# Attention units of a macaron block: the low halves of late weights after the scores' maxima, statistics and ScalarE's normalizations in halves

## The chip, the cores and the metric

The kernel runs on one core of one Trainium2 chip. The metric is the device time of one execution in microseconds. TensorE (PE in the rows) multiplies matrices, ScalarE (ACT) copies and exponentiates, VectorE (DVE) does elementwise work and reductions, GpSimd (POOL) helps, and SyncE (SP) issues the loads. Each engine takes its own instructions in order and waits on semaphores for the others.

## What is computed

A block in three parts on 2048 tokens of width 256 (8 sequences of 256): half a mixture of experts, attention, half a mixture of experts again, each on normalized input. The change lies in the attention:

```python
qi = hadamard((x @ wq_idx).reshape(B, S, Hi, Di))      # 16 index heads
ki = hadamard(x @ wk_idx)
I = einsum('bth,bhts->bts', x @ w_iw, relu(einsum('bthd,bsd->bhts', qi, ki)))
vals, idx = top_k(where(causal, I, NEG), 32)           # which keys each token sees
q, k, v = x @ wq, x @ wk, x @ wv                        # 16 heads, one k and v
p = softmax(scores of q with the 32 chosen k)
out = (p @ v).reshape(B, S, H * hd) @ wo
```

Products of float32 are made from halves: a weight or an activation is split into a high half (rounded for TensorE) and a low half (what is left), and three products of halves stand for one.

## The kernel before

`order()` (line 28) writes out by hand one list of stages. Each engine's block walks the whole list and emits its own part of every stage, so the list is the order of work on every engine at once. `tally` counts the stages, and the waits are made from those counts.

The tokens are worked in 4 groups of 512. In the attention there are 64 units U, 16 to a group (u is the place in the group). A unit takes two heads of one sequence. While unit U runs its attention, units up to 29 also carry one index head of a group two further on. What a unit's stages do, in the order of the list:

- `qi`: TensorE projects the next index head (six matmuls of 512 columns) into bank 0, ScalarE copies it twice (line 1085, `PA<-ps` and `RR<-ps`), VectorE subtracts for the low half (line 1281, `RR<-ps,RR` 128x256) and frees the bank.
- `scores`: TensorE multiplies q with k into banks 1 and 2. VectorE adds the mask and takes the maxima (line 1696, out `SP` and `NB`), which frees banks 1 and 2. ScalarE exponentiates (line 1250), four instructions with their sums.
- `wo` of unit U-3: twelve matmuls of 256 columns into banks 6 and 7.
- `l`: TensorE multiplies the index head with its keys, again into banks 1 and 2 (in the rows the first matmul is line 798, `ps<-PA`), so it waits until VectorE has read the scores. ScalarE takes the positive part into `R` (line 1242), VectorE sums it up (line 1657).
- `q`: the next head of q, in bank 0. `scale`: VectorE's reciprocal (line 1706), GpSimd's multiplications (line 1818). A step of the search for the 32 largest (`drip`, lines 1671 and 1674).
- `pv` of U-2 and `flip_p` of U-1: copies on ScalarE and subtractions of 128x512 and 128x384 on VectorE (line 1281).
- The end of the unit: what the change touches.

What stands at the end of units 0 to 12 before the change:

- `halve(32 + U)`: the dictionary `coming` gives for each late weight (wq 3 to 7, wo 1 to 7) the unit that issues its load and the unit that splits it. A `split` is ScalarE's copy into the high half (`RR<-stage`, line 1085) and at the same place of the list VectorE's subtraction for the low half (`RR<-stage,RR`, line 1281). The loads go through two shelves of the tile `stage`; a load waits until the low half of the weight that had its shelf is done. The splits stand in units 1 to 6 and 7 to 12 (one in each), the loads in units 0 to 11.
- `stats`, `rough` and `moments` of the last group (key "a", columns 12 to 15) at the end of units 1, 3 and 5: VectorE's means and variances (lines 1322, 1325), a first guess of the inverse root, and two steps of Newton.
- `centre` of that group on ScalarE at the end of unit 8, and of the groups with key "q" at the end of units 10 and 26: four instructions in one stage (line 1122). That of key "q" is written into `stage` and waits for all low halves that stand before it in the list.

The last group is transposed (`flip`) in unit 13, those of key "q" in units 14 and 30.

Of the kernel before, what the change touches and what calls it, by code (L numbers as in the profile page):

```python
# [30 lines left out]
def order():  # L31

    def bring(*names):
        return [("bring", q) for q in names]

    def split(eh, el, *names):
        return [("split", q, eh, el) for q in names]

    def high(*names):
        return [("hi", q, "act") for q in names]  # L40

    def low(*names):
        return [("lo", q, "dve") for q in names]
# [5 lines left out]
    def centre(key, g, at, *engines):  # L49
        k = 4 // len(engines)  # L50
        return [("centre", key, g, at, eng, k * i, k) for i, eng in enumerate(engines)]
# [4 lines left out]
    def scatters(n, *groups):  # L56
        return [st for r in range(2) for g in groups for st in
                [("tag", n, g)] * r + [("scatter", n, i, r) for i in range(4 * g, 4 * g + 4)]]

    def marks(n, *groups):  # L60
        return [("mark", n, g, 0) for g in groups]
# [99 lines left out]
    def fill3(s, late):  # L161
# [10 lines left out]
        elif (s, late) == (3, 1):  # L172
# [4 lines left out]
    yield ("attention",)  # L177
    yield from [("project", 0, 0), ("iw", 0), ("qi", 0, 0)]

    coming = {("wq", 0): (1, 3), ("wq", 1): (4, 6), ("wq", 2): (7, 9), ("wq", 3): (32, 33), ("wo", 1): (32, 34),  # L180
              ("wq", 4): (33, 35), ("wo", 2): (34, 36), ("wq", 5): (35, 37), ("wo", 3): (36, 38), ("wq", 6): (37, 39),
              ("wo", 4): (38, 40), ("wq", 7): (39, 41), ("wo", 5): (41, 42), ("wo", 6): (42, 43), ("wo", 7): (43, 44)}

    def halve(k):
        for name, (_, when) in coming.items():
            if k == when:
                yield from split("act", "dve", name)
        for name, (when, _) in coming.items():
            if k == when:
                yield from bring(name)  # L190

    def early(h):
        if h in (5, 9):
            yield ("stats", "a", h - 1, 4, h - 1)
        if h == 10:
            yield ("rough", "a", 4, 8, 4)
        if h == 11:
            yield ("moments", "a", 4, 8, 4)
        if h == 12:
            yield from centre("a", 1, 4, "act")  # L200
        if h == 13:
            yield ("flip", "a", 1, 3, 4)
        if h == 14:
            yield from centre("a", 2, 8, "act")
        yield from halve(h)
# [9 lines left out]
    def begin_topk(g):  # L215
        left.extend((what, g, b, r) for b in range(2) for what, r in [("best", r) for r in range(4)] + [("mask", 0)])
        return [("causal", g, 0), ("causal", g, 1)]

    def drip(k):
        out = left[:k]  # L220
        del left[:k]
        return out
# [3 lines left out]
    def ahead_to(U):  # L226
        while nextq[0] <= min(U, 63):
            yield ("q", nextq[0])
            nextq[0] += 1
# [13 lines left out]
    yield from drip(1) + [("project", 0, 2), ("iw", 2), ("qi", 2, 0)] + drip(1)  # L243
    yield from ahead_to(1)
    yield from begin_topk(1)
    yield from [("values", 0), ("l", 2, 0), ("qi", 2, 1)]

    later = scatters(1, 0, 1)[:8] + [None, None] + scatters(1, 0, 1)[8:]

    def prepare(U):  # L250

        stats = lambda g, i: [("stats", "m1", 4 * g + 2 * i, 2, 4 * g + 2 * i)]
        rest = lambda g, p: [(p, "m1", 4 * g, 4, 4 * g)]
        half = lambda g, i: [("half", "m1", g, i, 1 + i)]
        first, second, third = [], [], []
        for i, U0 in enumerate((20, 21, 35, 37, 51, 52)):
            if U == U0:
                first += stats(i // 2, i % 2)
        for i, U0 in enumerate((22, 39, 52)):
            if U == U0:  # L260
                first += rest(i, "rough")
        for i, U0 in enumerate((23, 41, 53)):
            if U == U0:
                first += rest(i, "moments")
        for g, begin in ((0, 24), (1, 42), (2, 53)):
            if U in (begin, begin + 1):
                third += centre("m1", g, 4 * g, "act", "act")[U - begin:U - begin + 1]
        for i, U0 in enumerate((34, 36, 44, 45, 55, 55)):
            if U == U0:
                second += half(i // 2, i % 2)  # L270
        for g, U0 in enumerate((46, 46, 56)):
            if U == U0:
                first.append(("logits", 1, g, 0 if g == 1 else 5))
        for q, begin in ((0, 47), (1, 57)):
            if U == begin:
                first.append(("pick", 1, q))
            elif U == begin + 1:
                first.append(("sel", 1, q))
            elif U == begin + 2:
                first += [("shift", 1, q), ("count", 1, q, 5), ("place", 1, q, 5)]  # L280
            elif U == begin + 3:
                first += [("choose", 1, q)] + (marks(1, 2) if q else marks(1, 0, 1))
                if q:
                    later.extend(scatters(1, 2)[:4] + [None, None] + scatters(1, 2)[4:])
        if U == 31:
            third.append(("blank", 1))
        elif 32 <= U < 40:
            third += [("clear", k) for k in (2 * U - 64, 2 * U - 63) if k < CLEARS]
        elif U == 62:
            third += [("refill", x) for x in range(3)]  # L290
        if U >= 50:
            third += [st for st in later[:2] if st]
            del later[:2]
        for i in range(3):
            if U == 32 + i:
                third += bring(("sh", 1, i))
            elif U == (50, 52, 58)[i]:
                third.append(("hi", ("sh", 1, i), "act"))
            elif U == (54, 56, 61)[i]:
                first.append(("lo", ("sh", 1, i), "dve"))  # L300
        return first, second, third

    for U in range(64):
        g, u = divmod(U, 16)
        gi, hi = divmod(U + 34, 16)
        idx = gi < NG
        first, second, third = prepare(U)
        if 0 < u < 14 and idx:
            yield ("qi", gi, hi)
        elif idx and (u == 15 or U == 16):  # L310
            yield ("qi", gi, hi - 1)
        yield ("scores", U)
        if U >= 32 and not first:
            yield from drip(1)
        yield from first
        if u == 15 and g + 1 < NG:
            yield ("project", 1, g + 1)
        if u == 14 and g < 2:
            yield ("flip", "q", g + 1, 3, 4)
        if U == 13:  # L320
            yield ("flip", "a", 3, 3, 4)
        if U >= 3:
            yield ("wo", U - 3)
        if u == 1 and U > 1:
            yield from [("pv", U - 2), ("values", g)]
        if U == 0:
            yield from ahead_to(2)
        if idx:
            if u == 14:
                yield from [("project", 0, gi), ("iw", gi)]  # L330
            elif u == 15:
                yield ("l", gi, 0)
            elif u == 0:
                yield from [("l", gi, 1), ("qi", gi, 2)]
            else:
                yield ("l", gi, hi)
        if 0 < u < 14 and U < 32 or u == 15 or U in (32, 33, 49):
            yield from ahead_to(U + 2 if U < 33 else U + 3)
        yield ("scale", U)
        if U < 32 and u < 13 and u != 1 and (u == 3 or u % 4 != 3):  # L340
            yield from drip(1)
        if U >= 2 and u != 1:
            yield ("pv", U - 2)
        yield from second
        if U:
            yield ("flip_p", U - 1)
        yield from ahead_to(U + 2 if U < 32 else U + 3)
        if idx and u == 0:
            yield ("l", gi, 2)
        yield from halve(32 + U)  # L350
        if U in (1, 3, 5):
            yield (("stats", "rough", "moments")[U // 2], "a", 12, 4, 12)
        if U == 8:
            yield from centre("a", 3, 12, "act")
        if u == 10 and g < 2:
            yield from centre("q", g + 1, 4 * g + 4, "act")
        if u == 13 and g < 2:
            yield from begin_topk(g + 2)
        yield from third
# [148 lines left out]
def macaron_kernel(nc, x, cst_in, row_in, gw_in, wsh_in, wex_in, wqi_in, ws_in, wiw_in, wq_in, wo_in, out):  # L508
# [7 lines left out]
    AX = mybir.AxisListType  # L516

    stages = list(order())
    at, whole = tally(stages)
    ctx = ExitStack()  # L520
# [1451 lines left out]
```

How the kernel before makes its waits and increments, by code:

```python
    def wait_ge(self, sem, value):  # L502
        if value > self.had.get(sem.name, 0):
            self.e.wait_ge(sem, value)
            self.had[sem.name] = value
# [206 lines left out]
        def settled(lane, m, g):  # L712
            num = min(8 * BATCHES[m][[g in q for q in BATCHES[m]].index(True)][-1] + 8 + NE - 1, NT)
            for k in range(4):
                lane.wait_ge(S[f"yst{k}"], 16 * (m * len(range(k, NT, 4)) + len(range(k, num, 4))))
# [68 lines left out]
        @block.tensor  # L785
# [34 lines left out]
            for st in stages:  # L820
                kind, a, n = st[0], st[1:], at[st]
                def free(bank):
                    t.wait_ge(S[f"bank{bank}"], n.get(("bank", bank), 0))
                    t.wait_ge(S["xres"], n.get(("emptied", bank), 0))
                if kind in ("flip", "half"):
                    key, g = a[0:2]
                    for done in CENTRED[key, g]:
                        t.wait_ge(*done)
                    t.wait_ge(S["ident"], 16)
                    src = NORMED[buffer(key, g)]
                    for dc, bank in enumerate(a[2:4]) if kind == "flip" else [a[2:4]]:
# [4 lines left out]
                        ins.then_inc(S["xt"], 1)  # L838
                elif kind == "warm":
                    t.wait_ge(S["warm"], 1)
                    for i in range(a[0]):
# [1 line left out]
                elif kind == "logits" and a[0] == 0:  # L843
                    m, g, bank = a
                    t.wait_ge(S["gates"], 2)
                    free(bank)
# [430 lines left out]
            def after(value):  # L1277
                t.wait_ge(S["dve"], value)
```

## Time and profile before

| | |
|---|---|
| median of 3 timed runs | 929.7 us (929.33 to 930.57) |
| profiled execution | 927.29 us, its span 925.5 us |
| TensorE's matmuls busy | 881.0 us, 95% of the span |
| VectorE, ScalarE, GpSimd busy | 685.4, 547.3, 394.6 us |
| mean granted TensorE clock | 0.992 of full speed |
| attention units 0 to 63 | from about 294 to 780 us of the span |

In rows of the timeline the first number is the start, the second the length, both in us; in brackets stands how long the engine was idle before it and which instruction ended the wait. A number after x counts merged instructions. Lines 1085 and 1281 are helpers, so the tiles tell which stage an instruction belongs to.

### The profile page before, as it was taken

Reading aid. Unit: us, or ns where it says so; the run is one execution under the profiler, and the core shown is the slowest. Engines: PE = TensorE matmul, PEld = TensorE weight load, DVE = VectorE, ACT = ScalarE, POOL = GpSimd, SP = SyncE. Lnnn points to the kernel's source line nnn. Section 1 sums busy time; section 2 is a strip of 40 time slices with the busy share of each in tenths; the row PEclk is TensorE's granted clock in tenths of the full one; section 3 lists DMA queues with packets and bytes.
Section 4 is the critical chain, followed back from the end, with each engine's and each line's share of the span. In section 5 each row is a group of like instructions: output and inputs, shape, how many; then the busy total and the mean of one; then the engine's idle time right before and its main releaser. Section 6 shows DMA issues by size and latency. Waiting matters only on the chain.

```text
span 925.5 us, 19094 instructions
## 1 busy us (share of the span) xinstructions
PE 881.0 (95%) x5846; PEld 787.8 (85%) x5847; DVE 685.4 (74%) x2388; ACT 547.3 (59%) x1586; POOL 394.6 (43%) x525
## 2 busy tenths in 40 slices
PE   8799999899999899989999999999999998999997
PEld 3478999788887788888899988999989997789996
DVE  7886667768797777766788676878678675847786
ACT  4454555457665566676666766667567774425562
POOL 0683687410000333323243344455428686126672
PEclk9999999999999999999999999999999999999999
DMA  9243896550000011000000000998000024624475
GB/s 348 94 138 126 311 352 218 120 115 23 1 1 1 15 33 35 13 23 2 1 2 1 1 1 1 307 308 223 1 1 35 30 89 171 270 70 127 133 243 173
DMA packets 52451, 96.26 MB, mean 104 GB/s; under 512 B 5824, under 2 KB 37184, under 8 KB 50304
## 3 DMA queue, kind: packets, MB, share of 16 engines
q1 hardware_dynamic: 44672, 73.20, 24.8%
q0 software_dynamic: 7680, 21.83, 7.5%
q8 instruction: 50, 0.82, 0.4%
q14 instruction: 49, 0.40, 0.2%
HBM read 44.99 MB, written 50.02 MB: 103 GB/s over the span
## 4 chain that ended last, share of the span: by engine, by line
PE 75%; DVE 15%; ACT 6%; issue 3%; DMA 0%; POOL 0%; DVEq 0%; ACTq 0%
PE ps L793 35%; PE ps L798 32%; DVE RR L1281 4%; PE ps L1042 3%; PE ps L951 2%; PE ps L921 2%; ACT SP L1250 2%; DVE PA L1657 1%; ACT RR L1085 1%; DVE st L1322 1%; DVE SP L1696 1%; PE ps L836 1%; DVE xl L1281 1%; DVE PA L1281 1%; DVE X L1281 1%
## 5 line engine op out<-in xcount | busy, mean ns | idle before, releaser
L1818 POOL TENSOR_SCALAR SP<-SP,RC 128x128 f32<-128x128 f32 (+1 forms) x256 | 193.6, 775 | 261.3 <-DVE RC L1706 261.1
L1281 DVE TENSOR_TENSOR RR<-ps,RR 128x256 fp32r<-128x256 f32 (+2 forms) x322 | 158.3, 525 | 74.3 <-ACT RR L1085 73.7
L798 PE MATMUL ps<-RR,RA 128*128 (+1 forms) x1002 | 176.6, 315 | 5.4 <-DVE RA L1281 4.2
L1250 ACT ACTIVATE SP<-SP,NB 128x128 f32<-128x128 f32 (+1 forms) x256 | 113.5, 444 | 76.0 <-DVE NB L1696 75.8
L1085 ACT ACTIVATE RR<-ps 128x256 fp32r<-128x256 f32 (+2 forms) x322 | 137.0, 469 | 28.3 <-PE ps L793 26.4
L798 PEld LDWEIGHTS ps<-RR,RA 128*128 128x128 f32 x1002 | 143.3, 189 | 11.8 <-issue 9.1
L793 PE MATMUL ps<-xh,RR 128*128 128x512 f32 x368 | 135.3, 412 | 0.0
L1657 DVE SCALAR_TENSOR_TENSOR PA<-R,IW,PA 128x128 f32<-128x128 f32 x240 | 84.8, 415 | 41.0 <-ACT R L1242 40.9
L1786 POOL DMA_INDIRECT yr<-FA,IDX x78 | 84.4, 1082 | 53.4 <-ACT FA L1085 16.7
L798 PE MATMUL ps<-RR 128*128 128x256 f32 x768 | 103.7, 285 | 3.0 <-DVE RR L1281 3.0
L798 PEld LDWEIGHTS ps<-RR 128*128 128x128 f32 x768 | 96.9, 191 | 4.0 <-DVE RR L1281 3.6
L793 PE MATMUL ps<-xh,RT 128*128 128x512 f32 x272 | 96.6, 401 | 0.2 <-DVE RR L1281 0.2
L793 PEld LDWEIGHTS ps<-xh,RR 128*128 128x128 f32 x368 | 71.3, 194 | 13.9 <-DVE RR L1281 0.2
L1085 ACT ACTIVATE QF<-ps 128x256 f32<-128x256 f32 x96 | 36.9, 384 | 66.4 <-PE ps L793 66.4
L793 PE MATMUL ps<-KIH,RR 128*128 128x256 f32 x256 | 76.2, 325 | 0.0
L793 PE MATMUL ps<-KH,RR 128*128 128x256 f32 x256 | 75.5, 323 | 0.0
L793 PE MATMUL ps<-xl,RR 128*128 128x512 f32 x184 | 74.2, 403 | 0.0
L1281 DVE TENSOR_TENSOR RA<-ps,RA 128x256 fp32r<-128x256 f32 x156 | 64.8, 417 | 8.8 <-ACT RA L1085 8.8
L1085 ACT ACTIVATE RA<-ps 128x256 fp32r<-128x256 f32 x156 | 59.4, 384 | 19.9 <-PE ps L921 19.6
L793 PE MATMUL ps<-RR,VH 128*128 128x512 f32 (+1 forms) x256 | 66.2, 340 | 0.1
L1242 ACT ACTIVATE R<-ps 128x384 f32<-128x384 f32 x128 | 58.8, 483 | 8.2 <-DVE VL L1281 2.7
L793 PEld LDWEIGHTS ps<-xh,RT 128*128 128x128 f32 x272 | 51.1, 188 | 10.2 <-DVE RR L1281 0.4
(238 smaller groups left out, 1867.2 us busy)
## 6 DMA issues: line engine op xcount, KB each, us to landing
xg<-stage SPq DMA_DIRECT2D x15, 1161.0 KB, 15.3
FA<-xg SPq DMA_DIRECT2D x78, 129.0 KB, 2.7
kept<-RR SPq DMA_DIRECT2D x8, 1216.0 KB
RR<-kept SPq DMA_DIRECT2D x8, 1216.0 KB, 10.8
X<-yr POOLq DMA_DIRECT2D x6, 512.0 KB, 5.6
RAW<-yr SPq DMA_DIRECT2D x6, 512.0 KB, 5.3
RAW<-wex_in SPq DMA_DIRECT2D x8, 352.0 KB, 9.7
RAW<-wsh_in SPq DMA_DIRECT2D x6, 384.0 KB, 9.1
```

The lines of the kernel that those rows point to most:

```text
L793: ins = e.matmul(o, a, c, start=first and i == 0, stop=last and i == len(seq) - 1, skip_group_check=True)
L798: return e.matmul(o, a, c, start=start, stop=stop, skip_group_check=True)
L921: ins = e.transpose(PS[bank][:, 128 * dc:128 * dc + 128], MOE[m].XS[j % NX][:, 128 * dc:128 * dc + 128], ident[:])
L951: ins = e.transpose(PS[bank][:, 128 * z:128 * z + 128], MOE[m].G[:, j % 2, 128 * z:128 * z + 128], ident[:])
L1042: ins = e.transpose(PS[3 + i][:, 128 * z:128 * z + 128], SP[:, k, i, 128 * z:128 * z + 128], ident[:])
L1085: return e.activation(o, i, ACT.Copy)
L1242: e.activation(R[:, b, :], PS[1 + b][:, 0:384], ACT.Relu).then_inc(S[f"bank{1 + b}"], 1)
L1250: ins = e.activation(SP[:, k, i, o:o + w], SP[:, k, i, o:o + w], ACT.Exp, scale=-1.0, bias=NB[:, k, 2 * i + z:2 * i + z + 1], accum_out=SM ...
L1281: return e.tensor_tensor(o, p, q, alu)
L1657: ins = e.scalar_tensor_tensor(Is, r, iw, Is, ALU.mult, ALU.add)
L1786: e.indirect_dma_start(out=YR[m], out_offset=bass.IndirectOffsetOnAxis(ap=IDX[:, j % 8:j % 8 + 1], axis=0), in_=MOE[m].YS[:, j % 4, :], in ...
L1818: ins = e.tensor_scalar(SP[:, k, i, o:o + w], SP[:, k, i, o:o + w], RC[:, k, 2 * i + z:2 * i + z + 1], None, ALU.mult)
```

## The change

The late weights leave `coming` for a list `pieces` in order of use. The load of the first stands before the units. At the end of unit U (0 to 11) ScalarE makes the high half of piece U; VectorE makes its low half in unit U+1 directly behind the scores' maxima. The load of piece U+2 is issued at the end of unit U (pieces 1 and 2 in unit 0). The last group's `stats` become two stages of two columns, in units 1 and 2, `rough` goes to unit 4 and `moments` to unit 6, all behind the maxima. ScalarE's `centre` of the last group is made in two halves at the end of units 8 and 9, those of key "q" in two halves at the end of units 11 and 12, and 27 and 28. No instruction is added or removed.

```diff
-    coming = {("wq", 0): (1, 3), ("wq", 1): (4, 6), ("wq", 2): (7, 9), ("wq", 3): (32, 33), ("wo", 1): (32, 34),
-              ("wq", 4): (33, 35), ("wo", 2): (34, 36), ("wq", 5): (35, 37), ("wo", 3): (36, 38), ("wq", 6): (37, 39),
-              ("wo", 4): (38, 40), ("wq", 7): (39, 41), ("wo", 5): (41, 42), ("wo", 6): (42, 43), ("wo", 7): (43, 44)}
+    coming = {("wq", 0): (1, 3), ("wq", 1): (4, 6), ("wq", 2): (7, 9)}
+    pieces = [("wq", 3), ("wo", 1), ("wq", 4), ("wo", 2), ("wq", 5), ("wo", 3), ("wq", 6), ("wo", 4), ("wq", 7), ("wo", 5),
+              ("wo", 6), ("wo", 7)]
...
-    yield from [("values", 0), ("l", 2, 0), ("qi", 2, 1)]
+    yield from [("values", 0), ("l", 2, 0), ("qi", 2, 1)] + bring(pieces[0])
...
         first, second, third = prepare(U)
+        if 1 <= U <= len(pieces):
+            first = low(pieces[U - 1]) + first
+        if U in (1, 2):
+            first.append(("stats", "a", 10 + 2 * U, 2, 10 + 2 * U))
+        elif U in (4, 6):
+            first.append((("rough", "moments")[U // 5], "a", 12, 4, 12))
...
-        yield from halve(32 + U)
-        if U in (1, 3, 5):
-            yield (("stats", "rough", "moments")[U // 2], "a", 12, 4, 12)
-        if U == 8:
-            yield from centre("a", 3, 12, "act")
-        if u == 10 and g < 2:
-            yield from centre("q", g + 1, 4 * g + 4, "act")
+        if U < len(pieces):
+            yield from high(pieces[U])
+        for k in {0: (1, 2), 11: ()}.get(U, (U + 2,)):
+            if k < len(pieces):
+                yield from bring(pieces[k])
+        if U in (8, 9):
+            yield from centre("a", 3, 12, "act", "act")[U - 8:U - 7]
+        if u in (11, 12) and g < 2:
+            yield from centre("q", g + 1, 4 * g + 4, "act", "act")[u - 11:u - 10]
```

## Rows read from the trace of the kernel before

**Rows 1.** The page, its first part: busy us, share of the span, instructions.
```profile
PE 881.0 (95%) x5846; PEld 787.8 (85%) x5847; DVE 685.4 (74%) x2388; ACT 547.3 (59%) x1586; POOL 394.6 (43%) x525
```

**Rows 2.** Waits of TensorE, 286 to 775 us: total us, times, longest us.
```profile
PE ps L798 <- DVE NB L1696: 10.1, 7, 2.8
```

**Rows 3.** Timeline of TensorE: the first matmuls of `l` in eleven units.
```profile
304.97 0.46 PE L798 MATMUL ps<-PA 128*128 128x128 f32 x2 [0.69 <-DVE NB L1696]
313.43 0.53 PE L798 MATMUL ps<-PA 128*128 128x128 f32 x2 [2.46 <-DVE NB L1696]
323.46 0.46 PE L798 MATMUL ps<-PA 128*128 128x128 f32 x2
333.04 0.46 PE L798 MATMUL ps<-PA 128*128 128x128 f32 x2 [1.11 <-DVE NB L1696]
351.62 0.46 PE L798 MATMUL ps<-PA 128*128 128x128 f32 x2 [1.65 <-DVE NB L1696]
377.73 0.46 PE L798 MATMUL ps<-PA 128*128 128x128 f32 x2 [0.95 <-DVE NB L1696]
397.50 0.46 PE L798 MATMUL ps<-PA 128*128 128x128 f32 x2 [2.84 <-DVE NB L1696]
405.80 0.39 PE L798 MATMUL ps<-PA 128*128 128x128 f32 x2
...
497.81 0.39 PE L798 MATMUL ps<-PA 128*128 128x128 f32 x2
506.04 0.39 PE L798 MATMUL ps<-PA 128*128 128x128 f32 x2
539.53 0.46 PE L798 MATMUL ps<-PA 128*128 128x128 f32 x2 [0.43 <-DVE NB L1696]
```

**Rows 4.** Windows around the lowered clock: us, busy by engine, PEclk, DMA share, GB/s.
```profile
310.30:313.70 3.40, 0.94 (x9) 0.77 (x8) 3.37 (x17) 0.59 (x3) 1.79 (x3) 1.00 0.33 80
313.70:317.10 3.40, 3.40 (x14) 3.09 (x13) 1.54 (x6) 2.35 (x10) 0.00 (x0) 0.50 0.01 2
665.30:668.70 3.40, 3.40 (x15) 3.21 (x15) 0.41 (x3) 0.00 (x0) 2.86 (x4) 0.50 0.00 0
```

**Rows 5.** Timeline of VectorE: the last group's statistics, `rough` and `moments`, ends of units 1, 3, 5.
```profile
310.62 1.39 DVE L1322 BATCH_NORM_STATS2 st<-X 128x6 f32<-128x256 f32 x4
312.05 0.38 DVE L1325 BATCH_NORM_AGGREGATE mv<-st 128x2 f32<-128x6 f32 x4
330.83 0.16 DVE L1284 TENSOR_SCALAR nt<-mv 128x4 f32<-128x4 f32 x1
331.84 0.17 DVE L1344 SCALAR_TENSOR_TENSOR nt<-nt 128x4 f32<-128x4 f32 x1
349.24 0.15 DVE L1281 TENSOR_TENSOR nt<-nt 128x4 f32<-128x4 f32 x1
350.43 0.17 DVE L1347 SCALAR_TENSOR_TENSOR nt<-mv,nt 128x4 f32<-128x4 f32 x1
```

**Rows 6.** Timeline of ScalarE: end of units 10 and 11, and the copy after it.
```profile
393.74 2.08 ACT L1122 ACTIVATE stage<-X,nt 128x256 f32<-128x256 f32 x4 [1.78 <-DVE RR L1281]
402.61 0.65 ACT L1085 ACTIVATE RR<-stage 128x512 fp32r<-128x512 f32 x1
403.42 0.38 ACT L1085 ACTIVATE PA<-ps 128x256 f32<-128x256 f32 x1 [0.16 <-PE ps L793]
```

**Rows 7.** Timeline of VectorE: low half of a weight (unit 11), maxima, next sums (unit 12).
```profile
403.54 0.68 DVE L1281 TENSOR_TENSOR RR<-stage,RR 128x512 fp32r<-128x512 f32 x1
404.68 0.42 DVE L1696 CUSTOM_DVE_ANT_0 SP<-ps,PA 128x256 f32<-128x256 f32 x1
407.42 1.41 DVE L1657 SCALAR_TENSOR_TENSOR PA<-R,IW,PA 128x128 f32<-128x128 f32 x4 [1.76 <-ACT R L1242]
```

**Rows 8.** DMA issues, KB, us to landing: quiet (280 to 410 us), then busy (90 to 170 us).
```profile
stage<-wo_in SPq DMA_DIRECT2D x6, 256.0 KB, 2.6
...
stage<-wqi_in SPq DMA_DIRECT2D x8, 256.0 KB, 4.2
```

More of the change, by code:

```diff
@@ L178, in order, with halve @@
     yield from [("project", 0, 0), ("iw", 0), ("qi", 0, 0)]
-    coming = {("wq", 0): (1, 3), ("wq", 1): (4, 6), ("wq", 2): (7, 9), ("wq", 3): (32, 33), ("wo", 1): (32, 34),
-              ("wq", 4): (33, 35), ("wo", 2): (34, 36), ("wq", 5): (35, 37), ("wo", 3): (36, 38), ("wq", 6): (37, 39),
-              ("wo", 4): (38, 40), ("wq", 7): (39, 41), ("wo", 5): (41, 42), ("wo", 6): (42, 43), ("wo", 7): (43, 44)}
-    def halve(k):
+    coming = {("wq", 0): (1, 3), ("wq", 1): (4, 6), ("wq", 2): (7, 9)}
+    def halve(h):
         for name, (_, when) in coming.items():
-            if k == when:
+            if h == when:
                 yield from split("act", "dve", name)
         for name, (when, _) in coming.items():
-            if k == when:
+            if h == when:
                 yield from bring(name)
+    pieces = [("wq", 3), ("wo", 1), ("wq", 4), ("wo", 2), ("wq", 5), ("wo", 3), ("wq", 6), ("wo", 4), ("wq", 7), ("wo", 5),
+              ("wo", 6), ("wo", 7)]
     def early(h):
```

## The prediction, made before the changed kernel was built or run

> **What bounds the kernel now.** I read the page's busy times first. TensorE's matmuls fill 881.0 us, 95% of the span [rows 1]. The change adds and removes no matmul, so all it can win is TensorE's idle time and time at a lowered clock. The second view is the list of TensorE's waits over the attention units. One line carries nearly everything: 7 waits, 10.1 us, for VectorE's maxima, which free banks 1 and 2 for the index product `l` [rows 2]. The third view is TensorE's timeline, which says in which units those waits lie. The reader is to see that they stand at the start of `l` in units 1, 2, 4, 6, 9, 11 and 27 (0.69, 2.46, 1.11, 1.65, 0.95, 2.84 and 0.43 us) [rows 3]. All but the first follow a unit whose end holds one of the pieces the change moves: statistics (end of unit 1), `rough` (3), `moments` (5), `centre` (8, 10 and 26). The fourth view, the windows, shows that after the 2.46 us wait the clock was granted at 0.50 for 3.4 us [rows 4], which is 1.2 instead of 2.4 GHz.
>
> The mechanism can be read from rows 5 to 7. At the end of a unit the order on VectorE is subtractions, a weight's low half, the extra piece, then the next unit's low half of `qi`, then the maxima. Whatever stands there pushes the maxima back one for one, and TensorE, after the twelve matmuls of `wo`, has nothing else to do. On the other side of the maxima VectorE waits anyway: 1.76 us for ScalarE, which first exponentiates and then makes `R` [rows 7]. The same wait stands in nearly all of units 1 to 12; one row stands for them.
>
> **What a unit costs when nothing waits.** From `l` to `l` an undisturbed unit takes 506.04 - 497.81 = 8.23 us, and it holds the same matmuls as units 3 to 11 [rows 3].
>
> **The change part by part.**
>
> *Units 3 to 12.* From 323.46 to 405.80 lie nine units in 82.34 us [rows 3]. Nine undisturbed ones would take 9 x 8.23 = 74.07 us. The difference, 8.27 us, is what VectorE's and ScalarE's extras cost there. The gaps of the four rows add to 6.55 us. The rest, 1.72 us, are shortfalls without a gap in brackets: a matmul that waited has lost its overlap with the one before it, and units with only a low half at their end are late by some tenths too. Moving the low halves removes those as well.
>
> *Unit 2.* Unit 2, like unit 1, has no `wo` ahead of `l`, so a wait is left even without extras: I take that of unit 1, 0.69 us. Gain 2.46 - 0.69 = 1.77 us [rows 3].
>
> *The clock.* From 313.43 to 323.46 a unit took 10.03 us [rows 3] with no gap in it: 1.80 us over 8.23. That is the stretch at 0.50 behind the gap [rows 4]. With 0.69 us instead of 2.46 us of idle time I take it to go away, since the gap of 0.69 us in unit 1 has no such stretch behind it. Bounds: 0 to 1.8 us of gain.
>
> The Trainium skill, page "TensorE: Matmul & The Clock Gate", section "Part 1: The HAM clock gate", has a monitor set the clock by how busy TensorE was lately. The stretch after the gap agrees [rows 4]. The other one does not so plainly: at 665.3 us the clock is at 0.50 too, and no wait of TensorE lies before it [rows 4]. By the page alone the first would go with the gap, as in my sum.
>
> *Unit 27.* 0.43 us of gap, and about 0.2 us of lost overlap as in the row of unit 9. Gain 0.6 us; ScalarE's half (below) finds idle time there.
>
> *What goes into the 1.76 us behind the maxima.* A low half is 0.68 us [rows 7]. With half of the statistics, (1.39 + 0.38) / 2 = 0.89 us [rows 5], units 1 and 2 take 1.57 us: covered. `rough` runs from 330.83 to 332.01, 1.18 us; with a low half 1.86 us, 0.10 over. `moments` runs from 349.24 to 350.60, 1.36 us; with a low half 2.04 us, 0.28 over [rows 5]. Queued behind are VectorE's sums and the low half of `q`, which frees bank 0 for the next `qi`. What is over has a unit's rest to be made good, because the low half of 0.68 us is gone from the end. I take 0; if it is not made good it is 0.4 us in all. Were there no cover at all, twelve low halves and the extras would be 12 x 0.68 + 1.77 + 1.18 + 1.36 = 12.5 us.
>
> *ScalarE's halves.* Four normalizations took 2.08 us, so a half is 1.04 us. At the end of units 8, 9 and 11 it follows a weight's high half. ScalarE had only 0.16 us of idle time between that high half (402.61) and the next copy (403.42) [rows 6]. So the copy of `qi` comes some 0.7 to 0.9 us later, and with it the maxima. In unit 12 the first pair's maxima ended at 405.10 and `l` began at 405.80, 0.70 us later, part of which TensorE needs to wake up [rows 3, 7]. What is left over is an estimated 0.15 to 0.35 us in each of three places: I take 0.5 us in all. At the end of units 12, 27 and 28 no high half stands before it. In unit 10 ScalarE also waited 1.78 us for VectorE's low half of a weight before it could overwrite `stage` [rows 6]. After the change the low halves waited for stand half a unit earlier, so that wait goes; it is part of the 2.84 us.
>
> *High halves a unit earlier.* In unit 0 a new one, 0.65 us, falls into the time before the next `qi` copy. In unit 12 one goes. Nothing in the sum.
>
> *The loads.* On SyncE only loads stand in this part of the list, so nothing is held up behind a waiting one. Each of the last three (wo 5, 6, 7) uses the shelf of its forerunner, and can start only behind that one's low half: just after the maxima. Its high half stands at the end of the same unit. In unit 12 the maxima ended at 407.42 - 1.76 = 405.66, so a low half would end at 406.34 [rows 7]; the high half of unit 11 began at 402.61 [rows 6], so one a unit later begins near 410.8: some 4.5 us for the load. A load took 2.6 us here, and 4.2 us where the queues were full [rows 8]. I take 2.6, as this stretch is quiet; both are covered.
>
> *Sum.* 8.27 + 1.77 + 1.80 + 0.6 - 0.5 = 11.9 us. Everything after these units waits on what they produce and on no fixed time, so the gain should reach the end. The sum is made against the profiled execution: 927.29 - 11.9 = 915.4 us. The timed runs' median lies 2.4 us above it, so from that: 929.7 - 11.9 = 917.8 us.
>
> **Rivals.**
>
> *The slow stretch stays or moves.* The waits go, but a stretch at 0.50 appears somewhere else, since units 0 to 2 keep gaps and since the one at 665.3 us follows no wait. Then the gain is 10.1 us and the time 919.6 us. On the other side the stretch at 665.3 may go too with the shifted start, for another 1.7 us: 916.1 us.
>
> *The work behind the maxima is not covered.* If ScalarE's `R` comes much earlier once the maxima are early, VectorE's idle time shrinks and the moved work pushes the sums, the low half of `q` and the next `qi`. If half of the moved 12.5 us lands on the path, the gain is about 5.7 us: 924.0 us. If all of it, nothing is won: 929.7 us, within 0.2%. Against it: ScalarE exponentiates for most of the 1.76 us whenever it starts, so the time moves along with the maxima.
>
> *The last three loads come late (slower).* If wo 5, 6 and 7 don't land by the end of their unit, ScalarE stands still with the copy of `qi` behind it, and so do the maxima and `l`. The cover is 4.5 us. To cancel 11.9 us a load would need 4.5 + 11.9 / 3 = 8.5 us. At 10 us each it would cost 3 x 5.5 = 16.5 us, so 934.3 us. Rows 8 show 2.6 and 4.2 us, half of that at most, so it is unlikely.
>
> **How the numbers follow.** Forecast 917.8 us, chance 0.60. Slow stretch stays, 919.6 us: 0.14. One more goes, 916.1 us: 0.12. Half covered, 924.0 us: 0.06. No cover, 929.7 us: 0.04. Late loads, 934.3 us: 0.04. The range goes from 914.3 (both stretches gone and no cost of ScalarE's halves, with a little room) to 921.3 us (slow stretch stays and the small costs are doubled or the unit's shortfalls remain). It leaves out 0.14. About 0.2%, 1.9 us, is what a measurement of this kernel can tell from no change. Faster by over that: 0.92; within: 0.04; slower: 0.04.
>
> **What would show each step.** In the profile after, TensorE's waits for VectorE's maxima should fall from 10.1 us to about 2, with 0.7 us in units 1 and 2 and none above 0.4 us elsewhere. From `l` to `l` units 3 to 12 should take 8.2 to 8.5 us. VectorE's low halves from `stage` should stand directly behind line 1696, and the idle time before line 1657 should fall from 1.76 us to about 1 in plain units and to nothing in units 4 and 6. The clock should stay at 1.00 around 314 us. No wait of ScalarE for a load of wo should appear. The prediction is wrong if TensorE's waits come back for bank 0 (low half of `q` late) or if units 8 to 12 stay above 9 us.

## The result, and the profile after

The changed kernel takes 917.3 us (median of 4 runs, 914.7 to 918.9) against 929.5 us before (928.7 to 930.6). The ratio is 0.9865, with a 95% interval of 0.9837 to 0.9894. The forecast was 917.8 us, in a range of 914.3 to 921.3. Run again on the chip of the last experiments it took 916.6 us (4 runs) against 928.4, ratio 0.9874 (0.9855 to 0.9892).

The profiled execution of the changed kernel took 914.69 us with a span of 912.9 us. It is the fastest of its four, as the profiled one of the kernel before (927.29 us) was faster than its timed ones.

The page's first part, and TensorE's waits over the attention units (286 to 775 us: total us, times, longest). These answer to [rows 1, 2]. The line numbers are 9 higher than before (807 for 798, 1290 for 1281, 1705 for 1696).

```profile
PE 878.3 (96%) x5846; PEld 785.2 (86%) x5847; DVE 685.6 (75%) x2388; ACT 547.0 (60%) x1586; POOL 393.8 (43%) x525
```

```profile
PE ps L807 <- ACT PA L1094: 1.4, 1, 1.4
PE ps L807 <- DVE NB L1705: 1.4, 2, 0.7
```

TensorE's waits for the maxima fell from 10.1 to 1.4 us. The two left are those of units 1 and 2, which have no `wo` ahead of the index product. The wait of 1.4 us for ScalarE (`PA`) lies in unit 0 and was there before too. TensorE's timeline shows them, and the same instruction in units 3, 4 and 12 with no wait. They answer to [rows 3].

```profile
305.80 0.46 PE L807 MATMUL ps<-PA 128*128 128x128 f32 x2 [0.70 <-DVE NB L1705]
312.50 0.46 PE L807 MATMUL ps<-PA 128*128 128x128 f32 x2 [0.69 <-DVE NB L1705]
320.81 0.39 PE L807 MATMUL ps<-PA 128*128 128x128 f32 x2
329.03 0.39 PE L807 MATMUL ps<-PA 128*128 128x128 f32 x2
...
395.39 0.46 PE L807 MATMUL ps<-PA 128*128 128x128 f32 x2
```

From unit 1 to unit 12 it is 395.39 - 305.80 = 89.59 us, where it was 405.80 - 304.97 = 100.83 us [rows 3]. That is 11.24 us of the 12.6 us by which the spans differ.

VectorE in unit 4 shows what now stands behind the maxima: the low half (line 1290, `RR<-stage,RR`), then `rough`, then the sums (line 1666). The rows answer to [rows 5, 7].

```profile
328.58 0.42 DVE L1705 CUSTOM_DVE_ANT_0 SP<-ps,PA 128x256 f32<-128x256 f32 x1
328.93 0.69 DVE L1290 TENSOR_TENSOR RR<-stage,RR 128x512 fp32r<-128x512 f32 x1
329.53 0.16 DVE L1293 TENSOR_SCALAR nt<-mv 128x4 f32<-128x4 f32 x1
...
330.55 0.17 DVE L1353 SCALAR_TENSOR_TENSOR nt<-nt 128x4 f32<-128x4 f32 x1
330.76 1.40 DVE L1666 SCALAR_TENSOR_TENSOR PA<-R,IW,PA 128x128 f32<-128x128 f32 x4
332.47 0.43 DVE L1290 TENSOR_TENSOR RR<-ps,RR 128x256 fp32r<-128x256 f32 x1 [0.31 <-ACT RR L1094]
```

The 1.76 us of idle time [rows 7] are filled to the last tenth, and the low half of `q` still waits 0.31 us for ScalarE afterwards: nothing was pushed. In a plain unit (10) the idle time has shrunk to 1.15 us:

```profile
379.06 0.69 DVE L1290 TENSOR_TENSOR RR<-stage,RR 128x512 fp32r<-128x512 f32 x1
380.89 1.41 DVE L1666 SCALAR_TENSOR_TENSOR PA<-R,IW,PA 128x128 f32<-128x128 f32 x4 [1.15 <-ACT R L1251]
```

ScalarE at the end of unit 11: high half, half of the normalization, and the `qi` copy straight behind it, without idle time. The rows answer to [rows 6].

```profile
392.07 0.65 ACT L1094 ACTIVATE RR<-stage 128x512 fp32r<-128x512 f32 x1
392.59 1.09 ACT L1131 ACTIVATE stage<-X,nt 128x256 f32<-128x256 f32 x2
393.58 0.39 ACT L1094 ACTIVATE PA<-ps 128x256 f32<-128x256 f32 x1
```

The loads land as quickly as before (2.6 us in [rows 8]), and ScalarE waits for none of them:

```profile
stage<-wo_in SPq DMA_DIRECT2D x6, 256.0 KB, 2.6
stage<-wq_in SPq DMA_DIRECT2D x4, 256.0 KB, 2.7
```

The windows of TensorE's clock (the third number from the end) show 1.00 where [rows 4] have 0.50: around unit 2, and also in and behind the router's narrow products. These run from 650.2 to 653.8 us now. Before, they ran from 661.6 to 665.2 us, and the stretch at 0.50 lay right behind them.

```profile
312.40:315.80 3.40, 3.30 (x19) 2.95 (x20) 3.16 (x13) 3.08 (x12) 0.53 (x1) 1.00 0.27 80
315.80:319.20 3.40, 3.40 (x25) 3.12 (x24) 3.37 (x12) 2.72 (x7) 2.58 (x4) 1.00 0.00 0
650.00:655.00 5.00, 5.00 (x47) 5.00 (x46) 2.32 (x14) 1.86 (x8) 0.53 (x1) 1.00 0.02 5
655.00:660.00 5.00, 5.00 (x35) 4.51 (x34) 2.42 (x7) 2.02 (x5) 2.46 (x4) 1.00 0.00 0
```

### The profile page after: what moved, and what is told of

It reads as the page before. It is cut to its first block, busy times and chain, and to the rows that moved or that the text cites. A ratio compares the mean times of both kernels' runs of the same rounds, so it can differ in the third digit from the quotient of the medians.

```text
span 912.9 us, 19095 instructions
## 1 busy us (share of the span) xinstructions
PE 878.3 (96%) x5846; PEld 785.2 (86%) x5847; DVE 685.6 (75%) x2388; ACT 547.0 (60%) x1586; POOL 393.8 (43%) x525
## 4 chain that ended last, share of the span: by engine, by line
PE 83%; DVE 10%; ACT 3%; issue 2%; DMA 0%; POOL 0%; DVEq 0%; ACTq 0%
PE ps L802 41%; PE ps L807 34%; PE ps L1051 4%; PE ps L960 2%; DVE RR L1290 2%; PE ps L930 2%; DVE st L1331 1%; PE ps L845 1%; ACT RR L1094 1%; DVE PA L1290 1%; DVE xl L1290 1%; ACT SP L1259 1%; DVE PA L1666 1%; DVE X L1290 1%; DVE FA L1290 1%
## 5 line engine op out<-in xcount | busy, mean ns | idle before, releaser
L807 PEld LDWEIGHTS ps<-RR,RA 128*128 128x128 f32 x1002 | 143.4, 189 | 12.6 <-issue 10.0
L802 PEld LDWEIGHTS ps<-xh,RT 128*128 128x128 f32 x272 | 51.1, 188 | 10.1 <-DVE RR L1290 0.4
```

Source lines behind the costliest of these rows:

```text
L802: ins = e.matmul(o, a, c, start=first and i == 0, stop=last and i == len(seq) - 1, skip_group_check=True)
L807: return e.matmul(o, a, c, start=start, stop=stop, skip_group_check=True)
```

## The experiments

Each is read by one measure, the time from the index product of one unit to that of the next. It is worked out from the starts of the same matmul in each kernel's timeline, as from [rows 3]. This is needed because differences of a few us can't be read from the timed medians. Those of e5, e6, e9, e7, e10 and e12 are of one run each: 918.3, 924.9, 923.2, 921.5, 919.0 and 920.0 us. The first four ran on another chip, on which the kernel before took 942.3 us (31 runs, 935.4 to 949.3) and TensorE's clock was lowered more often in the first 80 us. On every chip, units in which nothing waits take 8.22 to 8.24 us.

Time in us from the index product of the unit named to the next, and in all from unit 1 to unit 12:

| unit | before | changed | e1 | e2 | e3 | e4 | e5 | e6 | e9 | e7 | e8 |
|---|---|---|---|---|---|---|---|---|---|---|---|
| 1 | 8.46 | 6.70 | 7.66 | 6.76 | 8.47 | 6.75 | 6.69 | 6.72 | 6.72 | 6.70 | 6.64 |
| 2 | 10.03 | 8.31 | 8.30 | 8.47 | 9.85 | 8.48 | 8.32 | 8.30 | 8.32 | 8.31 | 8.15 |
| 3 | 9.58 | 8.22 | 9.10 | 8.48 | 9.50 | 8.47 | 8.24 | 8.79 | 8.31 | 8.23 | 8.23 |
| 4 | 8.47 | 8.23 | 8.30 | 8.47 | 8.47 | 8.47 | 8.44 | 8.85 | 9.66 | 8.22 | 8.23 |
| 5 | 10.11 | 8.23 | 9.43 | 8.82 | 10.11 | 8.83 | 8.24 | 9.21 | 8.71 | 8.23 | 8.22 |
| 6 | 8.47 | 8.22 | 8.31 | 8.48 | 8.48 | 8.48 | 9.02 | 8.86 | 10.05 | 8.23 | 8.23 |
| 7 | 8.30 | 8.23 | 8.22 | 8.30 | 8.30 | 8.30 | 8.24 | 8.32 | 8.56 | 8.22 | 8.23 |
| 8 | 9.34 | 8.36 | 9.33 | 9.33 | 8.39 | 8.39 | 8.36 | 8.78 | 8.37 | 8.36 | 8.23 |
| 9 | 8.47 | 8.43 | 8.31 | 8.48 | 8.47 | 8.47 | 8.44 | 8.86 | 8.93 | 10.08 | 8.22 |
| 10 | 11.30 | 8.30 | 9.33 | 11.30 | 8.47 | 8.47 | 8.32 | 8.84 | 8.75 | 9.06 | 8.23 |
| 11 | 8.30 | 8.36 | 8.30 | 8.30 | 9.61 | 9.60 | 8.36 | 8.44 | 8.64 | 9.98 | 8.23 |
| 1 to 12 | 100.83 | 89.59 | 94.59 | 95.19 | 98.12 | 92.71 | 90.67 | 93.97 | 95.02 | 93.62 | 88.84 |

### One part alone

**e1, the weights alone.** The changed kernel without the moves of the statistics and the normalizations.

```diff
-        if U in (1, 2):
-            first.append(("stats", "a", 10 + 2 * U, 2, 10 + 2 * U))
-        elif U in (4, 6):
-            first.append((("rough", "moments")[U // 5], "a", 12, 4, 12))
...
+        if U in (1, 3, 5):
+            yield (("stats", "rough", "moments")[U // 2], "a", 12, 4, 12)
+        if U == 8:
+            yield from centre("a", 3, 12, "act")
+        if u == 10 and g < 2:
+            yield from centre("q", g + 1, 4 * g + 4, "act")
```

> Of the change only the late weights are moved (loads, high halves, low halves behind the maxima); statistics, rough, moments and the normalizations stand as before. My theory (each extra costs what it pushes the next unit's maxima beyond about 0.55 us of slack that the moved low half leaves): over the changed kernel about 1.0 us in unit 2, 0.7 after rough, 0.9 after moments, 0.8 and 0.9 after the two normalizations (the 1.8 us wait of ScalarE for a low half is gone already) and 0.65 in unit 27, in all 5 us: 922 us, or 924 with a stretch at half clock in unit 2. Rival (only the extras were late, the low halves cost nothing where they stood): no gain over the kernel before but the wait of 1.8 us, 927.5 us.

Measured: 94.59 us, 5.00 over the changed kernel. The steps are 0.96 us (unit 1), 0.88 (3), 1.20 (5), 0.97 (8) and 1.03 (10), and 0.66 in units 26 and 27. From unit 1 to unit 28 that makes 5.58 us, where 5 were expected: `rough` and `moments` cost 0.2 and 0.3 us more than I had put them at. So the weights' move alone brings 100.83 - 94.59 = 6.24 us of the 11.24. Only 0.57 of it lies in plain units (4, 6, 7 and 9). Units 1, 3 and 5 give 1.96, since their extras no longer queue behind a low half, unit 10 gives 1.97, since its normalization no longer waits for one, and unit 2 gives 1.73, its time at half clock, which a gap of that length doesn't bring in every execution (see e12). The rival falls. The median was 939.5 against 942.3 us, ratio 0.9958 (0.9913 to 1.0003).

**e2, the statistics alone.** The kernel before with `stats`, `rough` and `moments` where the change has them.

```diff
         first, second, third = prepare(U)
+        if U in (1, 2):
+            first.append(("stats", "a", 10 + 2 * U, 2, 10 + 2 * U))
+        elif U in (4, 6):
+            first.append((("rough", "moments")[U // 5], "a", 12, 4, 12))
...
-        if U in (1, 3, 5):
-            yield (("stats", "rough", "moments")[U // 2], "a", 12, 4, 12)
```

> Of the change only statistics, rough and moments are moved behind the maxima; weights and normalizations stand as before. Theory: the gaps ahead of the index product in units 2, 4 and 6 go (1.77, 1.1 and 1.64 us), with them the stretch at half clock in unit 2 (1.8 us), the rest stays: 6.3 us gained, 923.2 us. Rival (the stretch at half clock has nothing to do with the 2.46 us gap): 4.5 us gained, 925.0 us, and the clock at 0.50 near 314 us of the profile.

Measured: 95.19 us, 5.64 less than before (expected 6.3). Unit 1 gives 1.70, unit 2 with its clock 1.56, unit 3 1.10 and unit 5 1.29. Unit 5 stays at 8.82 us, not 8.47, because the step of the search in that unit is the longer one, and the low half at the end meets it. No stretch at half clock lies behind unit 2. The median was 938.8 us, ratio 0.998 (0.9928 to 1.0031).

**e3, the halves alone.** The kernel before with the change's two `centre` places.

```diff
-        if U == 8:
-            yield from centre("a", 3, 12, "act")
-        if u == 10 and g < 2:
-            yield from centre("q", g + 1, 4 * g + 4, "act")
+        if U in (8, 9):
+            yield from centre("a", 3, 12, "act", "act")[U - 8:U - 7]
+        if u in (11, 12) and g < 2:
+            yield from centre("q", g + 1, 4 * g + 4, "act", "act")[u - 11:u - 10]
```

> Of the change only ScalarE's normalizations are halved and set one unit later; all else as before. Theory: the first pair gains 0.7 us and unit 27 0.65 us, but the pair of units 11 and 12 now waits twice for a low half at the end of its own unit (1.8 us each), so its 3.07 us become about 3.4: in all 1 us gained, 928.6 us, no difference that can be measured. Rival (halving alone removes the normalizations' price of 4.9 us): 925 us.

Measured: 2.7 us less from unit 1 to 12, of which the next interval gives back 1.5: it takes 10.62 us, and 9.13 before. From unit 10 to unit 13 it is 28.70 us, and 28.73 before, and the interval that starts at unit 13 is longer by 0.39 us. Halving the normalization of key "q" brings nothing as long as each half waits for a low half at its unit's end. In units 26 and 27, where no low half stands, it brings 0.65 us. From unit 1 to unit 28 the gain is 1.5 us, where 1 was expected. ScalarE's waits, 395 to 430 us of this kernel:

```profile
ACT SP L1250 <- DVE NB L1696: 3.9, 3, 1.8
ACT stage L1122 <- DVE RR L1281: 3.1, 2, 2.1
```

The second row is that wait: once 1.78 us before [rows 6], now twice, 3.1 us together. The pair of units 8 and 9, which waits for no low half, gained 0.95 us. The median was 941.5 us, ratio 0.9995 (0.9948 to 1.0043).

**e4, only the place of the low halves undone.**

```diff
-        if 1 <= U <= len(pieces):
-            first = low(pieces[U - 1]) + first
...
             yield from high(pieces[U])
+            yield from low(pieces[U])
```

> The changed kernel with each low half put back to the end of a unit, directly behind its own high half; all else as changed. Theory: some 0.2 us in each of the plain units 3 to 8 and 10, 0.4 in unit 2, and ScalarE's first half of the normalization in unit 11 waits 1.8 us for that unit's low half again: 3.3 us over the changed kernel, 920.6 us. Rival (the place of the low halves does not matter once the extras are gone): 917.3 us within half a microsecond.

Measured: 92.71 us, 3.12 over the changed kernel (expected 3.3). Plain units take 8.47 instead of 8.23 us, unit 5 takes 8.83, and unit 11 takes 9.60 because the normalization waits again. Place alone is worth 3.1 us here. The median was 934.0 us, 0.9917 (0.9869 to 0.9966) of the kernel before on that chip. The changed kernel itself has no run there.

The parts have to be added up to the first index product behind unit 13, where e3 has paid back what it gained in unit 10. Up to there (130.06 us before) they give 6.59, 5.65 and 0.84 us, 13.1 in all, and the change gives 11.53. e1 and e2 both remove the stretch at half clock of unit 2, 1.6 to 1.7 us, which counts twice in the 13.1. Beside that there is overlap both ways: without the low half at the end the extras cost less, and ScalarE's halves of key "q" bring nothing in unit 11 until it is gone.

### How much the place behind the maxima covers

**e5, three more instructions there.** In units 3 to 12 three statistics instructions, result unused, ahead of the low half.

```diff
+        if 3 <= U <= 12:
+            first = [("pad", U, 3)] + first
...
+                if kind == "pad":
+                    after(own[0])
+                    for i in range(a[1]):
+                        then(e.bn_stats(PAD[:, i, :], X[:, 12, :]))
```

> The changed kernel with three more statistics instructions on VectorE (1.08 us, their result unused) in each of units 3 to 12, directly behind the maxima and ahead of the low half. Theory (what stands behind the maxima is covered up to about 2.4 us): plain units hold 1.7 us there and stay at 8.2 to 8.4 us from one index product to the next; units 4 and 6, with rough and moments too, hold 2.9 to 3.1 us and grow by about 0.5 us each: 1 us over the changed kernel's profile in all. Rival (VectorE's total work is the bound now): 10 x 1.08 = 10.8 us over it.

Measured: 1.08 us over the changed kernel, though VectorE is busy 9.4 us longer (695.0 and 685.6 us on the pages). Plain units stay at 8.24 us. Unit 4 grew by 0.21 and unit 6 by 0.80.

**e6, the same instructions at the unit's end.**

```diff
+        if 3 <= U <= 12:
+            yield ("pad", U, 3)
```

> The same three instructions in the same units, but at the unit's end, where statistics, rough and moments stood before. Theory: each plain unit grows by 1.08 less 0.55 us of slack, about 0.6 us, those that end with half a normalization by about 0.3: 5 us over the changed kernel's profile, shown as TensorE waiting for the maxima at the start of the index product. Rival (place does not matter): the same as with the instructions behind the maxima.

Measured: 4.38 us over up to unit 12. The table holds nine of the ten ends; what stands at the end of unit 12 costs another 0.75 us in the interval that starts at unit 13. Up to the first index product behind it, ten times the same work costs 1.1 us in the one place and 5.2 us in the other (5 expected). A plain unit grows by 0.57 us (unit 3), not by the whole 1.08: about 0.5 us at the unit's end is slack. Unit 5, with the longer step of the search, grows by 0.98. TensorE's waits, 318 to 400 us, for e6 and then for e5:

```profile
PE ps L810 <- DVE NB L1712: 3.0, 7, 0.7
```

```profile
PE ps L805 <- DVE RR L1293: 0.5, 1, 0.5
```

**e9, six instructions behind the maxima.** The same edit as e5 with 6 for 3.

> Six more statistics instructions (2.16 us) behind the maxima in units 3 to 12, with the low half 2.8 us. Theory: the cover of about 2.4 us is passed; what gets late is the low half of q, so TensorE waits for bank 0 at the next index projection (line 802, ps<-xh), 0.3 to 0.4 us in plain units and about 1.5 us in units 4 and 6: 5.5 us over the changed kernel's profile. Rival (the cover ends at the 1.76 us of idle time): 10 x 1.0 plus the extras, 12 us.

Measured: 5.43 us over up to unit 12, and 0.69 in the next interval, together 6.1 where 5.5 were expected. Here the cover is passed, and the waits have another address (318 to 425 us):

```profile
PE ps L805 <- DVE RR L1293: 3.2, 5, 1.5
```

It is the projection (line 805, `ps<-xh`), which waits for bank 0. In unit 4 VectorE's queue shows why: with pads, low half and `rough` the sums begin 331.94 - 328.36 = 3.6 us after the last maxima, and the low half of `q` behind them.

```profile
327.94 0.42 DVE L1712 CUSTOM_DVE_ANT_0 SP<-ps,PA 128x256 f32<-128x256 f32 x1
328.28 2.05 DVE L1312 BATCH_NORM_STATS2 PAD<-X 128x6 f32<-128x256 f32 x6
330.25 0.67 DVE L1293 TENSOR_TENSOR RR<-stage,RR 128x512 fp32r<-128x512 f32 x1
...
331.94 1.40 DVE L1673 SCALAR_TENSOR_TENSOR PA<-R,IW,PA 128x128 f32<-128x128 f32 x4
333.27 0.41 DVE L1293 TENSOR_TENSOR RR<-ps,RR 128x256 fp32r<-128x256 f32 x1
```

```profile
333.74 0.50 PE L805 MATMUL ps<-xh,RT 128*128 128x512 f32 x1 [1.16 <-DVE RR L1293]
```

So the cover is more than the idle time of 1.76 us: 1.8 us of work is free (plain units of e5), 2.7 to 2.9 us cost 0 to 0.5 us (plain units of e9, unit 4 of e5), and 3.1 us (unit 6 of e5) cost 0.8.

### The late loads

**e7.** The loads of wo 5, 6 and 7 also wait for the reciprocal of the unit in which their high half stands.

```diff
+                        if name in (("wo", 5), ("wo", 6), ("wo", 7)):
+                            t.wait_ge(S["rc"], name[1] + 5)
```

> The changed kernel, but the loads of wo 5, 6 and 7 wait in addition for the reciprocal of the unit in which their high half stands, which comes 2.8 us after the low half they waited for. Theory (the late loads had over 1 us to spare): the load lands about 1.6 us after ScalarE gets to the high half; units 9 and 11, whose slack half a normalization uses already, grow by 1.6 us each and unit 10 by 0.8: 4 us over the changed kernel's profile. Rival (the loads were just in time in the changed kernel): 3 x 2.8 = 8.4 us over it.

Measured: 4.03 us over the changed kernel; units 9, 10 and 11 grew by 1.65, 0.76 and 1.62 us. ScalarE's waits, 360 to 400 us, show the mechanism of the slower rival:

```profile
ACT RR L1094 <- DMA stage<-wo_in: 4.5, 3, 1.5
```

Counted from the index product of their unit the three loads start 3.1, 3.1 and 3.5 us later than in the changed kernel (that of wo 5 at 4.1 instead of 1.0 us). ScalarE waits 1.5, 1.5 and 1.4 us, so they had 1.5 to 2.1 us to spare. Each microsecond beyond costs about a microsecond where half a normalization has used up the slack. The changed kernel's own trace has somewhat less, because one load took longer to land. From issue to high half it has 4.1, 4.1 and 4.4 us, and the loads land after 2.6, 3.1 and 2.5 us: 1.5, 0.9 and 1.9 us are to spare. The slowest of them, 378 to 382 us:

```profile
stage<-wo_in SPq DMA_DIRECT2D x1, 256.0 KB, 3.1
```

The rival's mechanism is real; its condition isn't met.

### The clock

**e10 and e12, the gap of unit 2 brought back.** The same kernel twice: seven statistics instructions at the end of unit 1.

```diff
+        if U == 1:
+            yield from [("pad", U, 4), ("pad", U, 3)]
```

> The changed kernel with seven statistics instructions (result unused) at the end of unit 1, which bring back a gap of about 2.5 us ahead of the index product of unit 2, and nothing else. Theory (the gap caused the stretch at half clock): a stretch at 0.50 of 3.4 us follows and unit 2 takes 10 us instead of 8.3, 3.5 us in all. Rival (the stretch had another cause or depends on where the gap falls in time): no stretch, unit 2 at 8.3 us, 1.8 us in all.

> The same kernel as e10 again, a second execution under the profiler. Theory: as in e10, a stretch at half clock behind the gap in both. Rival (it depends on where the gap falls in time): one of the two profiles, or neither, shows it.

Measured: in both the gap ahead of unit 2 is 2.4 us and unit 1 takes 8.39 us, 1.69 more. In e10 a stretch at half clock follows: the matmuls of 256 columns take 0.41 us in place of 0.28, and unit 2 takes 9.90 us.

```profile
312.41 0.28 PE L805 MATMUL ps<-KH,RR 128*128 128x256 f32 x1
315.08 0.68 PE L810 MATMUL ps<-PA 128*128 128x128 f32 x2 [2.39 <-DVE NB L1712]
...
315.77 0.41 PE L805 MATMUL ps<-KIL,RR 128*128 128x256 f32 x1
...
317.69 0.63 PE L805 MATMUL ps<-xl,RR 128*128 128x512 f32 x1
318.12 0.85 PE L805 MATMUL ps<-xh,RR 128*128 128x512 f32 x2
318.81 0.40 PE L805 MATMUL ps<-xl,RR 128*128 128x512 f32 x1
```

In e12 there is none, and unit 2 takes 8.31 us. With the kernel before and e3, three of the four profiles with this gap have the stretch. The longest gap of all, 2.84 us in unit 11, has none behind it in either of the two profiles that hold it (before and e2). In the profiles without these gaps the clock stays at 1.00 in these units. So the gap is what brings the stretch, but not in each execution, and what decides it isn't shown. The theory of e12 (a stretch in both) failed and its rival held.

### A version meant to be better

**e8.** Normalizations in quarters, and the two gaps of units 1 and 2 filled with work that stood behind the index product.

```diff
-        if U in (8, 9):
-            yield from centre("a", 3, 12, "act", "act")[U - 8:U - 7]
-        if u in (11, 12) and g < 2:
-            yield from centre("q", g + 1, 4 * g + 4, "act", "act")[u - 11:u - 10]
+        if 6 <= U <= 9:
+            yield from centre("a", 3, 12, "act", "act", "act", "act")[U - 6:U - 5]
+        if u in (10, 11, 12) and g < 2:
+            yield from centre("q", g + 1, 4 * g + 4, "act", "act", "act", "act")[u - 10:(u - 9 if u < 12 else 4)]
...
+        if U == 1:
+            yield ("flip_p", 0)
+        if U == 2:
+            yield ("pv", 0)
```

> A version meant to beat the changed kernel: ScalarE's normalizations of the last group in quarters at the ends of units 6 to 9, those of key q as one, one and two at the ends of units 10 to 12 and 26 to 28; the transposes of unit 1 and the p times v product of unit 2 stand ahead of the index product. Theory: a quarter (0.5 us) fits the slack, so units 8 to 11 fall from 8.30-8.43 to 8.23 us (0.5 us), and the two gaps of 0.7 us in units 1 and 2 are filled but for 0.1 (1.25 us): from the index product of unit 1 to that of unit 12 about 88.4 instead of 89.6 us, and 0.6 us before or in it: 1.7 us below the changed kernel. Rival (the copies that move ahead of R on ScalarE and VectorE push the sums): no difference.

> The changed kernel once more, on the same chip as the others of this call, as the base for them and a second profile. Theory: from the index product of unit 1 to that of unit 12 again 89.6 us; what differs from one execution to the next lies in the stretches at half clock outside these units. 12 us below the kernel before.

Measured: 88.84 us from unit 1 to 12, 0.75 less than the changed kernel's 89.59, which e11 repeated (89.58). The quarters bring their 0.53 us in full, as every unit from 8 to 11 takes 8.22 or 8.23. Filling the gaps brings 0.2 us of the 1.25 expected. The wait only moved, to the next projection:

```profile
317.41 0.50 PE L806 MATMUL ps<-xh,RT 128*128 128x512 f32 x1 [0.69 <-DVE RR L1294]
```

In time the two can't be told apart: 917.7 us (916.1 to 918.5) for e8 and 916.6 us (915.4 to 917.6) for the changed kernel, 4 runs each. e8's profile has one stretch at half clock more than e11's outside the units. That such stretches are what hides 0.75 us in the timed runs isn't shown.

## Why the prediction was right, point by point

**The mechanism** was as told. Work at the unit's end pushes the maxima and TensorE with them; behind the maxima it costs nothing up to 1.8 us. e5 and e6 show it with the same instructions in both places, e4 by undoing the place alone. One sentence of it was wrong: work at the end does not push "one for one". A low half of 0.68 us there costs 0.24 us in a plain unit (e4, unit 3), three statistics of 1.08 us cost 0.57 (e6). The sum didn't suffer, since it was made from measured intervals and not from lengths of instructions.

**The sum of the units.** For units 1 to 11 I had 1.77 + 1.80 + 8.27 - 0.5 = 11.34 us. Measured: 11.24.

- Unit 2's wait: 1.77 expected, 8.46 - 6.70 = 1.76 measured.
- The undisturbed unit of 8.23 us held in units 3 to 7.
- ScalarE's halves: 0.5 us expected. Units 8, 9, 10 and 11 stand 0.13, 0.20, 0.07 and 0.13 us over 8.23, together 0.53, and e8 brings all four to 8.23.
- `rough` and `moments` over the idle time by 0.1 and 0.3 us: taken at nothing, and nothing it was.
- Unit 27: 0.6 expected, 0.66 measured (units 26 and 27).

**The clock** is the step that was less sure than its place in the sum said. I took 1.8 us to go away, and in the profile 1.72 did (unit 2, 10.03 and 8.31 us). But e12 shows that the gap has no such stretch in some executions, so the kernel before need not pay it each time. The 1.8 us is a price paid in three of four profiles. The error is hidden by what the prediction didn't have.

**What it didn't have.** The interval that starts at unit 13 is 0.37 us shorter. I had noted that a high half leaves unit 12 ("In unit 12 one goes"), and put it at nothing; the low half leaves the end of that unit too. That end stands ahead of the transposes of key "q", and TensorE's wait for VectorE there shrinks (before, then after):

```profile
421.03 1.06 PE L836 MATMUL ps<-ident,stage 128*128 128x128 f32 x8 [0.36 <-DVE RR L1281]
```

```profile
410.33 1.06 PE L845 MATMUL ps<-ident,stage 128*128 128x128 f32 x8 [0.16 <-DVE RR L1290]
```

e1 and e4, whose unit 12 ends without these halves too, take 19.75 and 19.73 us in this interval like the changed kernel (19.73); e2, where they stand, takes 20.09 like the kernel before. The interval of unit 12 is 0.08 longer.

Outside these units the two profiles differ in what comes and goes by execution. Behind unit 28 the changed kernel is 1.23 us shorter, as the stretch at 665 us [rows 4] is missing. Up to unit 1 it is 0.83 us later. Its additional stretch at half clock at 24 us is not the reason: behind it, at 31.70 and 31.68 us, the same matmul starts in both. The lag builds up between 93 and 140 us, in the first part's experts, at a granted clock of 1.00 in both profiles. In the ten profiles outside e1 to e4 the index product of unit 1 starts anywhere from 304.8 to 309.8 us; why isn't shown. The sum closes: 11.24 - 0.08 + 1.04 + 1.23 - 0.83 = 12.60 us, where 1.04 is units 13 to 27. So the terms of the units were right (11.9 told, 11.24 + 0.66 = 11.90 measured). That the median came within half a microsecond of the forecast is partly luck: the four runs spread over 4.2 us, and the terms not told add up to 0.70 us in the profile.

**The rivals.** "The slow stretch stays or moves" came true in part: one at 24 us is new, the one at 665 us is gone. The latter is missing in three profiles (the changed kernel, e11 and e10) and there in the other eleven. e10 and e12 are the same kernel and differ in it, so it comes and goes by execution. That the change has no part in it isn't shown: both profiles of the changed kernel lack it, and the one profile of the kernel before has it. The lack of cover didn't occur; e9 shows that it sets in about 1 us later than the idle time suggests. Late loads didn't occur. I had put the cover of a load at 4.5 us against 2.6 of landing, 1.9 to spare; it was 0.9 to 1.9, so the loads were up to 1 us nearer to being late than I thought.

**In the expectations of the experiments** the theory of e12 was wrong (a stretch in both executions). The other misses were smaller: e1 (5.58 for 5), e2 (5.64 for 6.3), where I had not seen that unit 5 has the longer step of the search, e3 (1.5 for 1), e9 (6.1 for 5.5), and e8, where I reckoned with one wait of TensorE and not with the one behind it.

## What to carry to other kernels

In a list order shared by all engines, look for the place where an engine waits anyway for a neighbour that is still at work on what it just got, and put loose work there. Work at the end of a round stands ahead of what the busiest engine needs first. Cost each piece by what it pushes, not by its length: the same 1.08 us of VectorE's work cost 0.1 us a unit behind the maxima and 0.5 us at the end. A normalization split in pieces only helps if no piece waits for something that is made at the same late place.

## What the runs showed of the hardware that was not expected

- A matmul that had to wait costs more than its gap: the unit behind it is 0.07 us longer (8.30 and not 8.23), and about 0.16 us of overlap with the matmul before is lost (e1, unit 8: 9.33 us less the gap of 0.94 is 8.39). Units with a hidden wait and no gap in brackets took 8.47 us, not 8.23.
- The same kernel with the same gap of 2.4 us had TensorE at half clock for 3.4 us behind it in one profile and not in the other (9.90 and 8.31 us for the unit). A gap of 2.84 us had it in none of two.
- The router's 32 products of 16 and 8 columns, 3.6 us in which TensorE is busy without a pause, come with a stretch at half clock of 3.4 or 6.8 us in 11 of 14 profiles. It starts among them or up to 1.3 us behind the last. The two later runs of 16 such products (1.8 us each, about 65 and 130 us later) have none in any of the 14.
